# Down projection: one 512-column matmul for rounded weights and remainder, added on the way out of PSUM

## The reference

```python
x = x + _L0_attn_ref(_layernorm(x), w_qkva, gamma)      # rmsnorm, projections, sigmoid gate, scan, q * y
def _swiglu(x_flat, wg, wu, wd):
    g = jnp.einsum('nd,edh->enh', x_flat, wg)
    u = jnp.einsum('nd,edh->enh', x_flat, wu)
    h = jax.nn.silu(g) * u
    return jnp.einsum('enh,ehd->end', h, wd)
top_vals, top_idx = jax.lax.top_k(logits, TOP_K)         # 2 of 7, softmax of the two
mixed = jnp.einsum('end,ne->nd', routed_out, combine)
mixed = mixed + jnp.mean(shared_out, axis=0)
x = x + mixed
```

## Time and profile before

| | |
|---|---|
| median of 3 runs | 1073.99 us (1073.85 to 1074.45) |
| the profiled execution | 1074.53 us, its span 1072.8 us |
| TensorE busy | 1050.7 us, 98% of the span |
| VectorE, ScalarE, GpSimd busy | 639.1, 582.1, 573.9 us |
| mean granted TensorE clock | 0.996 of full speed |

### The profile page before, as it was taken

How to read it: one execution, slowest core, us unless ns; L and a number is a source line. 1 busy time by engine, 2 the same in 40 slices (tenths; PEclk the granted TensorE clock), 3 DMA queues, 4 the chain that set the end, 5 groups by cost and what they waited for, 6 DMA issues and landing times.

```text
span 1072.8 us, 22463 instructions
## 1 busy us (share of the span) xinstructions
PE 1050.7 (98%) x8429; PEld 1033.7 (96%) x8429; DVE 639.1 (60%) x1058; ACT 582.1 (54%) x849; POOL 573.9 (53%) x309
## 2 busy tenths in 40 slices
PE   6999999999899999999999999999999999999998
PEld 5788999999899999999999999999999999999998
DVE  5997677765654545554555545555555555465655
ACT  3555433225466666666666666676666666433232
POOL 2226200005677777777777777777777776500000
PEclk9999999999999999999999999999999999999999
DMA  8333204004676777777777777777777777354241
GB/s 298 85 89 89 79 7 142 11 2 138 197 252 218 254 229 257 237 257 238 248 244 227 254 227 250 237 257 239 251 247 227 254 224 231 82 150 138 73 123 39
DMA packets 166630, 195.81 MB, mean 183 GB/s; under 512 B 79545, under 2 KB 151490, under 8 KB 156354
## 3 DMA queue, kind: packets, MB, share of 16 engines
q1 hardware_dynamic: 158496, 174.62, 50.9%
q0 software_dynamic: 7296, 19.93, 6.0%
q10 hardware_dynamic: 802, 0.79, 0.2%
HBM read 166.99 MB, written 28.31 MB: 182 GB/s over the span
## 4 chain that ended last, share of the span: by engine, by line
PE 90%; DVE 6%; ACT 2%; issue 1%; DMA 0%; POOL 0%; DVEq 0%; ACTq 0%; POOLq 0%
PE ps L813 56%; PE ps L830 28%; PE ps L723 3%; DVE y_sb L941 2%; PE ps L709 1%; DVE w_lo L1149 1%; DVE hT_lo L901 1%; PE ps L788 1%; PE ps L734 1%; ACT w_hi L602 1%; DVE stats L881 1%; DMA resid<-in_L_attn_x_dram 0%; ACT z_all L536 0%; DVE ps L1162 0%; ACT h_hi L617 0%
## 5 line engine op out<-in xcount | busy, mean ns | idle before, releaser
L813 PE MATMUL ps<-xs_hi,w_hi 128*128 128x256 f32 x1728 | 490.6, 284 | 4.2 <-DVE ps L1162 3.4
L813 PE MATMUL ps<-xs_hi,w_lo 128*128 128x256 f32 x1728 | 490.0, 284 | 0.0
L813 PE MATMUL ps<-xs_lo,w_hi 128*128 128x256 f32 x1728 | 489.9, 284 | 0.0
L466 POOL TENSOR_TENSOR w_lo<-raw,w_hi 128x2048 fp32r<-128x2048 f32 x81 | 385.5, 4760 | 125.0 <-ACT w_hi L602 116.7
L813 PEld LDWEIGHTS ps<-xs_hi,w_hi 128*128 128x128 f32 x1728 | 332.9, 193 | 4.8 <-DVE ps L1162 3.6
L813 PEld LDWEIGHTS ps<-xs_lo,w_hi 128*128 128x128 f32 x1728 | 332.7, 193 | 0.0
L813 PEld LDWEIGHTS ps<-xs_hi,w_lo 128*128 128x128 f32 x1728 | 332.7, 193 | 0.0
L612 ACT ACTIVATE silu<-ps 128x512 f32<-128x512 f32 x216 | 128.3, 594 | 226.4 <-PE ps L813 226.2
L1162 DVE TENSOR_TENSOR ps<-ps,silu 128x512 f32<-128x512 f32 x188 | 131.5, 699 | 195.9 <-ACT silu L612 187.2
L830 PE MATMUL ps<-w_hi,h_hi 128*128 128x256 f32 x864 | 245.2, 284 | 2.3 <-DVE h_lo L1167 2.3
L830 PE MATMUL ps<-w_hi,h_lo 128*128 128x256 f32 x864 | 245.0, 284 | 0.0
(11 more groups left out here) (138 smaller groups left out, 687.8 us busy)
## 6 DMA issues: line engine op xcount, KB each, us to landing
raw<-in_L_ffn_w_up_dram SPq DMA_DIRECT2D x38, 1024.0 KB, 5.2
raw<-in_L_ffn_w_gate_dram SPq DMA_DIRECT2D x38, 1024.0 KB
raw<-in_L_ffn_w_down_dram SPq DMA_DIRECT2D x38, 1024.0 KB, 5.5
sorted_rows<-x_stage SPq DMA_DIRECT2D x38, 256.0 KB, 2.2
x_rows<-sorted_rows SPq DMA_DIRECT2D x152, 64.0 KB, 5.3
got<-expert_rows SPq DMA_DIRECT2D x32, 256.0 KB, 3.6
resid<-in_L_attn_x_dram SPq DMA_DIRECT2D x8, 512.0 KB, 6.7
z_rows<-z_all SPq DMA_DIRECT2D x8, 512.0 KB, 2.9
```

Source lines behind the costliest of these rows:

```text
L466: pool.tensor_tensor(w_lo[buf][:, k, :], raw[:, k, :], w_hi[buf][:, k, :].bitcast(F32), ALU.subtract).then_inc(wlo_ready[k], 1)
L813: last = pe.matmul(o, w[:, part, at[kd]:at[kd] + P], xx[:, u, kd, :], start=i == 0, stop=i == len(terms) - 1)
```

## The change

The remainder of the weights now lies beside the rounded weights in one tensor (`w_both`, the same bytes at the same place), so that one matmul with `h_hi` as the stationary operand can stream both: 256 columns of `hi`, which go to the first half of the bank, and 256 of `lo`, which go to the second half. The third product, `h_lo` by `hi`, stays a matmul of 256 columns into the first half. The two halves hold two partial sums, which are added on the way out: in shared slots DVE adds first one half to `resid` and then the other; in routed slots ACT copies the second half to `y_rows`, and DVE adds the first half to it.

```diff
-            t, at = place(f"w_hi{b}", [P, 3, WPART], F32R)
-            w_hi.append(t)
+            t, at = place(f"w_both{b}", [P, 2, 3, WPART], F32R)
+            w_both.append(t)
+            w_hi.append(t[:, 0])
+            w_lo.append(t[:, 1])
             w_at.append(at)
-            w_lo.append(sb(f"w_lo{b}", [P, 3, WPART], F32R))
...
                 if r is not None:
                     act.wait_ge(down_psum, n + 2)
                     act.wait_ge(y_free, r)
-                    act.activation(y_rows[:, u, :, :], ps[:, 4:6, 0:D], ACT.Copy
-                                   ).then_inc(down_free, 1)
+                    act.activation(y_rows[:, u, :, :], ps[:, 4:6, D:2 * D], ACT.Copy).then_inc(y_half, 1)
...
                     for j in (2 * p, 2 * p + 1):
                         for t in range(ST):
-                            terms = ((h_hi, hi), (h_hi, lo), (h_lo, hi))
-                            for i, (hh, w) in enumerate(terms):
-                                last = pe.matmul(ps[:, 4 + t, 0:D], hh[:, j, t * P:(t + 1) * P],
-                                                 w[:, 2, j * D:(j + 1) * D],
-                                                 start=j == 0 and i == 0,
-                                                 stop=j == JH - 1 and i == len(terms) - 1)
+                            pe.matmul(ps[:, 4 + t, :].rearrange("p (b d) -> p b d", d=D),
+                                      h_hi[:, j, t * P:(t + 1) * P],
+                                      both[:, :, 2, j * D:(j + 1) * D],
+                                      start=j == 0, stop=False)
+                            last = pe.matmul(ps[:, 4 + t, 0:D], h_lo[:, j, t * P:(t + 1) * P],
+                                             hi[:, 2, j * D:(j + 1) * D],
+                                             start=False, stop=j == JH - 1)
...
                     rows = resid[:, bass.ds(shared, ST), :]
-                    dve.tensor_tensor(rows, ps[:, 4:6, 0:D], rows, ALU.add).then_inc(down_free, 1)
+                    dve.tensor_tensor(rows, ps[:, 4:6, 0:D], rows, ALU.add).then_inc(half_added, 1)
+                    dve.wait_ge(half_added, (n if back is None else n - NB0 + SA) + 1)
+                    dve.tensor_tensor(rows, ps[:, 4:6, D:2 * D], rows, ALU.add).then_inc(down_free, 1)
                     dve.wait_ge(down_free, n + 2)
+                if routed:
+                    dve.wait_ge(y_half, n - SA + 1)
+                    dve.tensor_tensor(y_rows[:, u, :, :], ps[:, 4:6, 0:D], y_rows[:, u, :, :], ALU.add
+                                      ).then_inc(down_free, 1)
```

More of the change, by code:

```diff
@@ L88, in preln_scan_moe_kernel @@
         raw = sb("raw", [P, 3, WPART])
-        w_hi, w_lo, w_at = [], [], []
+        w_both, w_hi, w_lo, w_at = [], [], [], []
         for b in range(2):
-            t, at = place(f"w_hi{b}", [P, 3, WPART], F32R)
-            w_hi.append(t)
+            t, at = place(f"w_both{b}", [P, 2, 3, WPART], F32R)
+            w_both.append(t)
+            w_hi.append(t[:, 0])
+            w_lo.append(t[:, 1])
             w_at.append(at)
-            w_lo.append(sb(f"w_lo{b}", [P, 3, WPART], F32R))
         h_hi, h_at = place("h_hi", [P, JH, SLOT], F32R)
@@ L255, in preln_scan_moe_kernel @@
         down_free = sem("down_free")
+        half_added = sem("half_added")
+        y_half = sem("y_half")
         y_out = [sem("y_out0"), sem("y_out1")]
@@ L799, in slot @@
                         pe.wait_ge(wlo_ready[k], m + 1)
-                hi, lo = w_hi[buf], w_lo[buf]
+                both, hi, lo = w_both[buf], w_hi[buf], w_lo[buf]
                 for p in range(PAIRS):
@@ L1151, in split_lo, with slot @@
                 ins.then_inc(wlo_ready[k], 1)
-            def slot(n, u, nth, up=None, shared=None, back=None, early=False, between=()):
+            def slot(n, u, nth, up=None, routed=False, shared=None, back=None, early=False, between=()):
                 for p in range(PAIRS):
@@ L1213, in _ @@
                 for u in range(2):
-                    slot(i * 2 + (SA + u), u, i * LD + LD * (R0 + 1 + u), up=i * 2 + (3 + u))
+                    slot(i * 2 + (SA + u), u, i * LD + LD * (R0 + 1 + u), up=i * 2 + (3 + u), routed=True)
             B0 = NB0 // 2
-            slot(NB0 - 2, 0, LD * B0, up=ROUTED + 1)
-            slot(NB0 - 1, 1, LD * (B0 + 1))
+            slot(NB0 - 2, 0, LD * B0, up=ROUTED + 1, routed=True)
+            slot(NB0 - 1, 1, LD * (B0 + 1), routed=True)
             dve.wait_ge(mix_ready, TOP)
```

## The result

The kernel with the change takes **1068.99 us** (median of 8 runs, 1068.62 to 1070.47), the kernel before on the same chip 1073.03 us (8 runs, 1071.57 to 1074.45): a ratio of 0.9966 (0.9955 to 0.9976), some 4.0 us faster. That is inside the range and 2.7 us above the forecast. The profiled execution took 1068.97 us, with a span of 1067.2 us; before it was 1074.53 and 1072.8.

The account below looks back on a forecast made before the run. TensorE's matmul issue pace was taken to bound nearly every slot. Terms: -9.79 (51 slots) + 0.64 (slot 2) + 0.73 (slot 8) + 0.73 (end) = -7.7 us, giving 1066.3 us; range 1063.8 to 1069.6.

Parts of the forecast that it names:

- What a merged pair saves: TensorE's down part: one 512-column matmul saves 0.012 us (0.010 to 0.014) against two of 256; 0.19 us a slot.
- rival B: Down part: no gain per instruction, a pair saves 0 to 0.0025 us; 1074.0 to 1075.9 us; 8 in 100.
- Where the saving is swallowed: Slots 6, 7 and 53 do not pass the saving on; the other 51 give 9.8 us.
- Routed slots' adds at nothing: 38 routed slots: VectorE's second add, counted 0.73 us, is covered by about 2 us and costs nothing.
- Slot 2: VectorE runs behind there; TensorE stalls 0.27 us at pair 2 and 0.37 at pair 3, together +0.64 us.
- Slot 8 and the end: Second adds of slot 7 (lengthening TensorE's wait in slot 8) and of slot 53 cost +0.73 us each.
- I take it that each of the two keeps its one slow stretch: TensorE's waits in slots 6 and 8 each keep one following stretch at granted clock 0.50, as before.
- The price of 1.7 us for a stretch: Behind the wait in slot 8, the next 48 matmuls take 7.49 us instead of 5.76, 1.7 us more.
- A: Moving operand: the two-piece source is read slower, 0.033 us a pair lost, 1103 us; 5 in 100.
- C: More waits or a further slow stretch, say behind slot 8's longer wait; 1068.0, up to 1070 us; 15 in 100.
- D: More gain: excess at 512 columns no larger than at 256, no slot 2 stalls; 1063.2 to 1064.7 us; 10 in 100.
- the 2.5 ns beyond the columns: Skill's rule for matmuls in a stream: by it a merged pair would save 0.0025 us; the prediction saw no such row.

Follow-up runs that it names:

- run 8: Changed kernel with two 512-column matmuls, then two of 256, in turn (the row tiles of one hidden block side by side); 1067.19 us, one run.
- run 9: Changed kernel with two wide matmuls into one PSUM bank, then two narrow ones into the same bank; 1064.86 us, one run.
- run 10: Changed kernel with two wide, then two narrow matmuls, the narrow ones in reverse order of the banks; 1067.62 us, one run.
- merge_alone: Run 1: changed kernel without the second adds, so only the first half of each bank leaves PSUM; 1068.03 us, 0.9953 of the kernel before.
- one_run: Same as run 4: changed kernel with down weights and remainders side by side per hidden block; 1068.96 us, 0.9966 of before.
- run 3: The change in slots 8 to 52 alone, the other slots as in the kernel before; 1067.65 us, 0.9954 of before.
- adds_alone: Run 2: three 256-column matmuls as in the kernel before, but with the changed kernel's ACT and VectorE steps; 1076.31 us, 1.0024 of before.
- run 4: Changed kernel with down weights and remainders side by side per hidden block, so the 512 columns are neighbours; 1068.96 us, 0.9966 of before.
- run 5: Changed kernel with four 512-column matmuls, then four of 256, instead of in turn; 1068.25 us, 0.9957 of before.
- run 11: The change in slots 8 to 52 alone, with two wide and two narrow matmuls in turn; 1064.71 us, 0.9920 of before.
- run 7: The change in slots 8 to 52 alone, all 16 wide matmuls of a slot first, then its 16 narrow ones; 1082.78 us, 1.0088 of before.
- Run 6: Changed kernel with the third product also over 512 columns, so the down part has only wide matmuls; 1153.44 us, one run.
- inner_slots: Same as run 3: the change in slots 8 to 52 alone, the other slots as in the kernel before; 1067.65 us, 0.9954 of before.

## Why the prediction was right and wrong

The mechanism was right, one size was not, and that the time lies in the range is in part luck: a gain of 7.7 us was forecast, and 4.0 were measured.

- **What a merged pair saves: the mis-sized term.** "The merged one then saves 0.012 us by the first, 0.010 by the second"; it saved 0.0075 (17.16 against 17.28 in 16 pairs), below the lower end. The rows of 512 columns in `project` stand in a stream of their own width, and the prediction itself noted under rival B that they hold no change between 512 and 256. That condition belonged into the bound, and not only into a rival. 51 x 16 x 0.0045 = 3.7 us is what it took from the gain. The 0.012 was the right number for two wide ones in a row (runs 8 to 10), not for a wide one between narrow ones (merge_alone, one_run).
- **Where the saving is swallowed: borne out.** With 51 slots the profiled executions and the runs 1 and 3 add up to within 0.5 us.
- **Routed slots' adds at nothing: right.** 0.69 us, 2.19 us of cover, the scatter right behind the split; in adds_alone the period did not move.
- **Slot 2: right.** 0.30 and 0.39 us, forecast 0.27 and 0.37.
- **Slot 8 and the end: right.** The wait is 4.2 us (forecast about 4.3), the last add comes 0.73 after the first.
- **"I take it that each of the two keeps its one slow stretch": wrong as put.** The stretch behind a wait comes in some executions of one kernel and not in others: those of before with a mean granted clock of 1.00 took 1070.3 to 1071.6 us, those with 0.998 took 1071.9 to 1073.2, those with 0.996 took 1073.5 to 1074.8. The prediction's sum was made against an execution that had two (of before), and the one of after had one, which flattered it by 1.5 us; without that its span would have been 1068.7 and its time 1070.4, above the range's end of 1069.6, and the two executions of after with a mean clock of 0.995 and 0.996 did take 1070.47 and 1070.39. So the range was met with the help of a clock that it had not reckoned with. The medians hold such executions mixed, and their difference of 4.0 us agrees with the 4.1 of the terms. The price of 1.7 us for a stretch was too high as well: the 48 matmuls of slot 8 take 6.11 us at the upper clock and not 5.76, which leaves 1.38.
- **Rivals.** A is out: one_run shows that the jump costs nothing. The sentence of the Trainium skill on non-contiguous access patterns (PSUM — Partial Sum Buffer, section Specifications (TRN2)) is about PSUM. Each matmul here writes a stretch of PSUM without a step, so no run here tests it. The jump is in the moving operand, two runs of 256 columns, and there it costs nothing, 17.16 us a slot with and without it. B is out as priced, since 0.0075 is three times its upper bound, but its doubt about the change of width was the part that came true. C's longer wait came at its forecast length; the traces lean to its dearer stretch without showing it. Behind a wait of 4.1 to 4.3 us all seven profiles (after, runs 2, 4, 5, 8, 9 and 10) had a slow stretch, and in three of them (runs 2, 9 and 10: 8.17, 7.97 and 8.24 us for the 48 matmuls) it cost 1.9 to 2.1 us. Behind 3.4 or 3.5 us three profiles had one (before, runs 1 and 11), at 1.4 us, and two had none (runs 3 and 7). Run 6 had one behind 2.6 us. These are single executions of different kernels. D did not come.

The prediction set the 2.5 ns beyond the columns (the Trainium skill, TensorE: Matmul & The Clock Gate, section Back-to-back issue gap) against a stream like this one. That section calls it the gap of an isolated matmul and says that a stream of weight loads and matmuls has another spacing; each matmul here has a weight load of its own. These runs have 0.120 - 0.1067 = 0.013 us at 256 columns and, with 0.2275 between the 0.227 of run 6 and the 0.228 of the earlier trace rows, 0.2275 - 0.2133 = 0.014 at 512. The measurement decides: in streams of one width the excess stands once per instruction, nearly the same at either width.

**What stays open** is why widths in strict turn cost 0.0042 us a pair more than two and two, and four and four 0.0025 more. The number of changes, the bank, the two-piece source and VectorE's adds are excluded by runs; what it is was not found. All orders have the same weight loads and the same columns. But which load runs beneath which matmul changes with the order, and that was not varied by itself.

## What to carry to other kernels

A duration read from a stream of equal instructions is a bound only for such a stream: where a change mixes two shapes, their mixture is an unknown of its own, and its cost can depend on the order in which they stand, so try two or three orders that mean the same. Merging pays for each instruction saved and costs an add for each slot's way out, so do it only where the added work is covered: here slots 8 to 52 in pairs of two gave 8.8 us, and the change everywhere, in turn, 4.0. Before moving short instructions behind long ones, ask what they cover: in run 7 they were the time in which `h_lo` came.

## What the runs showed of the hardware that was not expected

- Matmuls of 512 and 256 columns, each with its own weight load: a 512 and a 256 take 0.3483 us in groups of two and two, 0.3508 in groups of four, and 0.3525 in turn. Behind a long run of 256 columns the first five wide ones took 0.232 to 0.234 us each, later ones 0.227.
- A moving operand in two runs of 256 columns that lie a tensor apart is streamed as fast as a contiguous one (755.04 us in 44 slots for both).
- The same wait of TensorE, 2.3 us in slot 6 or 3.4 in slot 8, was followed by a stretch at a granted clock of 0.50 in one execution (before) and by none in another (inner_slots). A stretch cost 1.4 to 1.5 us there, and up to 2.1 behind waits of 4.1 to 4.3 us.
